# Attention kernel: the blocks that ScalarE copies move from the row-score banks into the ring of score banks

## What is computed

```python
A1 = einsum('bhqd,bhkd->bhqk', Q1, K1) * scaling      # 16 heads, head part of 16 values
A2 = einsum('bhqd,bhkd->bhqk', Q2, K2) * scaling
attn = softmax(A1) - lamb * softmax(A2)
out = einsum('bhqk,bhkd->bhqd', attn, V)
out = layernorm(out.reshape(B, S, DIM) @ Wo) * gamma + beta
```

## Time and profile before

| | us |
|---|---|
| median of 3 runs | 4075.53 (4073.76 to 4076.94) |
| the profiled execution, its own time | 4072.35 |
| its span, from the first to the last instruction | 4070.5 |
| row-score reductions from the prologue's first to the last | 368.6 to 3204 |
| PE busy in the span | 3755.0 |
| DVE busy | 3159.8 |
| ACT busy | 2786.5 |

### The profile page before, as it was taken

One profiled execution on the slowest core, in us unless ns is written; L12 is line 12 of the kernel. 1 busy time (PEld: TensorE's weight loads), 2 busy tenths in 40 slices (PEclk: granted clock), 3 DMA queues, 4 the chain that ended last, 5 costly groups with the idle time before them and its releaser, 6 DMA issues. The chain is left out here.

```text
span 4070.5 us, 63429 instructions
## 1 busy us (share of the span) xinstructions
PE 3755.0 (92%) x23714; PEld 1470.7 (36%) x23714; DVE 3159.8 (78%) x5580; ACT 2786.5 (68%) x3267; POOL 1103.3 (27%) x1520
## 2 busy tenths in 40 slices
PE   6998599999999999999999999999999859899999
PEld 4773122222222222222222222222222236578888
DVE  5457599989999998999999899999999413344444
ACT  3441388888888887888888788888888936522221
POOL 3211013204113212310411231032123157662420
PEclk9997699999999999999999999999999979999999
DMA  5546601111011111111111111111101069832320
GB/s 181 188 162 234 221 29 43 38 49 50 27 48 40 38 48 36 42 38 50 32 37 51 32 38 40 48 32 45 43 22 43 22 235 333 254 115 64 100 83 21
DMA packets 224694, 330.88 MB, mean 81 GB/s; under 512 B 29298, under 2 KB 165237, under 8 KB 219781
## 3 DMA queue, kind: packets, MB, share of 16 engines
q1 hardware_dynamic: 173988, 244.61, 18.5%
q0 software_dynamic: 18432, 50.36, 3.8%
q10 hardware_dynamic: 31968, 31.85, 2.4%
HBM read 169.34 MB, written 156.34 MB: 80 GB/s over the span
## 5 line engine op out<-in xcount | busy, mean ns | idle before, releaser
L1616 DVE TENSOR_REDUCE arena<-psum 128x1 f32<-128x512 f32 x4096 | 2558.5, 681 | 218.3 <-PE psum L1282 200.9
L1470 ACT ACTIVATE arena<-psum,exp_scale 128x1024 f32<-128x1024 f32 x2048 | 2157.7, 1110 | 298.8 <-PE psum L1320 288.9
L1282 PE MATMUL psum<-arena 48*128 48x512 f16 x4096 | 1314.1, 394 | 157.9 <-ACT arena L1430 55.9
L1336 PE MATMUL psum<-arena 128*32 128x512 f32 x8200 | 1107.1, 612 | 1.2 <-ACT arena L1470 0.6
L1282 PEld LDWEIGHTS psum<-arena 48*128 48x128 f16 x4096 | 317.1, 93 | 1808.4 <-DVE arena L1616 1487.0
L1320 PE MATMUL psum<-arena 50*128 50x512 f16 x4096 | 901.7, 384 | 15.9 <-ACT arena L1470 9.2
L1510 POOL TENSOR_TENSOR arena<-arena 128x16 f32<-128x16 f32 x129 | 28.4, 220 | 2123.7 <-DVE arena L1626 2123.7
L991 ACT ACTIVATE mix_arena<-psum,mix_arena 128x1024 f32<-128x1024 f32 x64 | 71.3, 1114 | 329.6 <-DVE mix_arena L1011 329.6
L1336 PEld LDWEIGHTS psum<-arena 128*32 128x32 f32 x8200 | 162.2, 108 | 258.0 <-issue 256.5
L1320 PEld LDWEIGHTS psum<-arena 50*128 50x128 f16 x4096 | 214.0, 95 | 94.1 <-ACT arena L1470 79.4
L894 POOL DMA_INDIRECT mix_arena<-scratch_sorted_y,mix_arena x192 | 181.7, 946 | 235.6 <-PE psum L946 169.1
(11 more groups left out here) (168 smaller groups left out, 3315.4 us busy)
## 6 DMA issues: line engine op xcount, KB each, us to landing
arena<-scratch_split SPq DMA_DIRECT2D x762, 64.0 KB
scratch_split<-route_arena SPq DMA_DIRECT2D x64, 512.0 KB, 2.8
scratch_sorted_x<-arena ACTq DMA_DIRECT2D x60, 512.0 KB, 7.4
leaf_arena<-scratch_sorted_x SPq DMA_DIRECT2D x60, 512.0 KB, 5.8
scratch_sorted_y<-leaf_arena SPq DMA_DIRECT2D x60, 512.0 KB, 4.1
leaf_arena<-in_leafw SPq DMA_DIRECT2D x3, 5128.0 KB, 18.9
arena<-in_x SPq DMA_DIRECT2D x18, 512.0 KB, 4.7
scratch_sum<-arena SPq DMA_DIRECT2D x18, 512.0 KB, 3.0
```

The costliest lines, as they stand in the source:

```text
L1282: nc.tensor.matmul(aux_bank[bank], ring[at, slot, 0, m, qt * P:(qt + 1) * P], ring[at, slot, 1, m, c * CH:(c + 1) * CH], start=True, stop=True
L1336: last = nc.tensor.matmul(value_bank[32 * j:32 * j + 32, :], vaug[:, batch % 2, kt, 2 * pair + j % 2, :], prob[:, step % 2, j, :], start=k ...
L1470: nc.scalar.activation(prob[:, step % 2, 2 * h:2 * h + 2, :], score[:, 2 * h:2 * h + 2, :], ACT.Exp, scale=exp_scale[:, s % 2, s // 2:s // ...
L1616: nc.vector.tensor_reduce(halfmax[:, odd, 2 * m + h, qt, c:c + 1], aux_bank[bank], AX.X, ALU.max).then_inc(bank_used[bank], 1)
```

## The change

The extras leave the ring of three banks. Every exp of a pair and every extra becomes an "item"; the items are numbered in the order in which ACT takes them, and item g is put in slot g mod 2. A slot is one of the two pairs of score banks; an extra uses the first bank of the pair. Item g may be filled when item g - 2 has been read (`wait_slot`). So the pair of banks of m = 0 and m = 1 is no longer fixed, and alternates after each extra. The three banks `aux_bank` hold row scores alone: row score r goes to bank r mod 3 and waits for row score r - 3. The two semaphores `score_full`, `extra_full` become `item_full`, and ACT's reads of either kind count in `item_read`. The order of the instructions on each engine stays: in a step scores 0, row 0, scores 1, row 1, values, row 2, extras, row 3.

```diff
-    score_full, exp_done = sem("score_full"), sem("exp_done")
+    item_full, item_read = sem("item_full"), sem("item_read")
...
-    aux_half = [a.bitcast(F16) for a in aux_bank]
+    item_bank = [ps[:, 2 * n * CH:(2 * n + 1) * CH] for n in range(2)]
+    item_half = [a.bitcast(F16) for a in item_bank]
...
+    item_keys = [("shift", 0)]
+    row_start = [MAXIMA + 4 * AHEAD]
+    for n in range(SETS):
+        i, s = divmod(n, PER_BATCH)
+        for step in range(STEPS):
+            item_keys += [("exp", n, step, 0), ("exp", n, step, 1)]
+            item_keys += [(kind, n, step, number) for kind, number in extras(s, step, i == LAST)]
+            row_start.append(row_start[-1] + len(rows(s, step, i == LAST)))
+    item_keys += [("end", kind, number) for kind, number in EPILOGUE]
+    item_at = {key: g for g, key in enumerate(item_keys)}
+
+    def wait_slot(eng, g):
+        eng.wait_ge(item_read, g + 1)
+
+    def wait_full(eng, g):
+        eng.wait_ge(item_full, g + 2)
+
+    def wait_item(eng, g):
+        eng.wait_ge(item_read, g + 3)
+
+    def wait_row_bank(eng, r):
+        eng.wait_ge(bank_used[r % AUX], r // AUX + 1)
...
             def scores(i, s, step, m):
                 c, kt = step // TT, step % TT
-                g = 2 * (STEPS * s + step)
+                g = item_at["exp", i * PER_BATCH + s, step, m]
+                slot = g % 2
...
-                pe.wait_ge(exp_done, i * SCORES + (g + m + 1))
+                wait_slot(pe, g)
                 for h in (1, 0):
...
-                    last = nc.tensor.matmul(score[:, 2 * m + h, :], ...
+                    last = nc.tensor.matmul(score[:, 2 * slot + h, :], ...
-                last.then_inc(score_full, 1)
+                last.then_inc(item_full, 1)
...
-            def use(i, k, s, step, kind, number):
-                bank = k % AUX
-                wait_free(pe, k)
+            def extra(i, s, step, kind, number):
+                n = i * PER_BATCH + s
+                g = item_at[kind, n, step, number]
+                wait_slot(pe, g)
...
                         scores(i, s, step, 0)
-                        if early:
-                            use(i, k, s, step, *todo[0])
+                        row(0)
                         scores(i, s, step, 1)
-                        if early:
-                            use(i, k + 1, s, step, *todo[1])
+                        row(1)
...
-                        for n in range(early, len(todo)):
-                            use(i, k + n, s, step, *todo[n])
-                        k += len(todo)
+                        row(2)
+                        for kind, number in extras(s, step, tail):
+                            extra(i, s, step, kind, number)
+                        row(3)
```

More of the change, by code:

```diff
@@ L1134, in rows @@
         return [] if tail and target >= PER_BATCH else [("max", first + n) for n in range(4)]
[L1136 to L1142, removed]
     PROLOGUE = [("max", 0, n) for n in range(MAXIMA)] + [("max", 1, n) for n in range(2 * AHEAD)] + \
@@ L1148, in attention_stage, with wait_row_read, shift_item, o_item @@
     LAST = BATCH - 1
[L1149 to L1177, removed]
+    item_keys = [("shift", 0)]
[16 more added lines that the diff above has]
+        eng.wait_ge(bank_used[r % AUX], r // AUX + 1)
+    def wait_row_read(eng, r):
+        eng.wait_ge(bank_used[r % AUX], r // AUX + 2)
+    def shift_item(n):
+        return item_at["shift", 0] if n == 0 else item_at["shift", n - 1, SHIFT_STEP, 0]
+    def o_item(n, c):
+        return item_at["o", n, 5 if c else 11, c]
+    def group_item(i, kind, h, number):
+        s, step = GROUP_PLACES[f"{kind}{h}"][number]
+        return item_at[f"{kind}{h}", i * PER_BATCH + s, step, number]
     def group_end(i, h, kind):
-        places = GROUP_PLACES[f"{kind}{h}"]
-        return place(i, *places[-1], f"{kind}{h}", len(places) - 1)
+        return group_item(i, kind, h, len(GROUP_PLACES[f"{kind}{h}"]) - 1)
     with nc.Block() as block:
@@ L1224, in _ @@
             load_set(2)
-            wait_read(sp, PROLOGUE.index(("shift", 0, 0)))
+            wait_item(sp, shift_item(0))
             place_shift(0)
@@ L1255, in body @@
                     if n + 1 < SETS:
-                        wait_read(sp, place(i, s, SHIFT_STEP, "shift", 0))
+                        wait_item(sp, shift_item(n + 1))
                         place_shift((n + 1) % RING)
@@ L1361, in use @@
                 elif kind == "o":
-                    turn_o(number, i * (2 * PER_BATCH) + (2 * s + (0 if number else 1)), bank)
+                    turn_o(number, 2 * n + (0 if number else 1), g % 2)
                 elif kind in ("turn0", "turn1"):
-                    turn_group(i, int(kind[-1]), number, bank)
-                elif kind in ("out0", "out1"):
+                    turn_group(i, int(kind[-1]), number, g % 2)
+                else:
                     h = int(kind[-1])
[L1367 to L1374, removed]
+                    wait_item(pe, group_item(i, "turn", h, number // 2))
+                    groups[h].project(nc, item_bank[g % 2], number).then_inc(item_full, 1)
@@ L1376, in body, with row @@
             def body(i, tail):
-                k = START[i]
                 for s in range(PER_BATCH):
                     for step in range(STEPS):
-                        todo = uses(s, step, tail)
-                        early = 2 if rows(s, step, tail) else 0
+                        target = row_target(s, step)[0]
+                        first = row_start[STEPS * (i * PER_BATCH + s) + step]
+                        todo = rows(s, step, tail)
+                        def row(n):
+                            if n < len(todo):
+                                number = todo[n][1]
+                                if number == 0:
+                                    pe.wait_ge(slot_in[target % RING], 16 * LOADS * ((i * PER_BATCH + target) // RING + 1))
+                                wait_row_bank(pe, first + n)
+                                row_scores(number, target % RING, (first + n) % AUX)
@@ L1445, in read_group @@
                         act.wait_ge(groups[h].stored, i * 16 + 1)
-                    groups[h].read_projected(nc, aux_bank[bank], number).then_inc(bank_used[bank], 1)
+                    groups[h].read_projected(nc, item_bank[slot], number).then_inc(item_read, 1)
             act.wait_ge(lam_dots, 1)
             nc.scalar.activation(lam_exp, lam_dot, ACT.Exp).then_inc(lam_exps, 1)
-            act.wait_ge(extra_full, 1)
-            read_shift(0, PROLOGUE.index(("shift", 0, 0)) % AUX)
-            def read(i, s, kind, number, bank):
+            wait_full(act, shift_item(0))
@@ L1461, in body @@
             def body(i, tail):
-                k = START[i]
                 for s in range(PER_BATCH):
+                    n = i * PER_BATCH + s
                     for step in range(STEPS):
[L1465 to L1470, removed]
+                        act.wait_ge(value_done, i * VALUES + (STEPS * s + step + 1))
+                        for m in range(2):
+                            g = item_at["exp", n, step, m]
+                            wait_full(act, g)
+                            nc.scalar.activation(prob[:, step % 2, 2 * m:2 * m + 2, :], score[:, 2 * (g % 2):2 * (g % 2) + 2, :],
@@ L1476, in body @@
                             copy_values(i, s - 1, 1)
[L1477 to L1481, removed]
+                        for kind, number in extras(s, step, tail):
+                            g = item_at[kind, n, step, number]
+                            wait_full(act, g)
+                            read(i, s, kind, number, g % 2)
             for i in range(BATCH):
@@ L1626, in invert @@
                 nc.vector.reciprocal(linv[:, c], osum[:, c, :, :, HD]).then_inc(inverse_ready, 1)
-            for k, (kind, n, number) in enumerate(PROLOGUE):
-                if not is_row(kind):
+            row = 0
+            for kind, n, number in PROLOGUE:
+                if kind == "shift":
                     continue
-                dve.wait_ge(rows_full, rows_before[k] + 1)
-                read_max(n, number, k % AUX)
+                dve.wait_ge(rows_full, row + 1)
+                read_max(n, number, row % AUX)
```

138 lines of the change are left out of this document (74 added, 64 removed).

## The result

The changed kernel takes 4111.28 us (median of 4 runs, 4108.88 to 4115.11) against 4074.65 us before (4 runs, one more than in the table above). The ratio is 1.0091, 95% interval 1.0075 to 1.0107: slower by 37 us, where 36 and a median of 4111 were forecast. The profiled execution spans 4107.0 us against 4070.5.

A forecast was written before the change was run, and what follows sets the result against it. DVE was taken to set the pace, with PE's chain counting around extras. Extras +39.8 us and prologue -4 gave +36 on 4075.5: a median of 4111 us, own range 4098 to 4124, overall range 4078 to 4130.

The forecast's parts named there:

- What sets the pace: Attention stage: DVE sets the pace; around extras PE's chain delays it; plain steps stay 2.49 us, DVE waits about 39 more.
- The wait moves one place forward: PE's step after an extra: scores 1, not row 1, wait for ACT's copy; row 1 runs 0.28 us after it.
- Rival 1: Steps after extras: the freed banks win, row 1 no longer waits for a copy; 4039 us in all; chance 8%.
- The price of one extra: Row 1 after an extra: +0.12 us per "o", 0.11 projected, 0.22 turned block or shift; sum 39.8 us.
- The prologue: End of prologue: 43.70 us stall ahead of 14 reductions goes, scores start 5 us earlier, half clock takes 1: -4 us.
- Rival 4: The clock falls at shifts: 81 us more, 4192; with a few such places, 4125 to 4150; chance 7%.
- The rule of the Trainium skill: PE's idle before scores 1 of a shift, 0.7 us: small idles between groups cycling through PSUM banks can make the clock oscillate.
- Rival 2: No net change: DVE slack takes up 0.1 to 0.2 us, leaving prologue and some shifts; 4071 to 4083; chance 7%.

The follow-up runs named there:

- experiment 1: Changed kernel with row score 1 ahead of scores 1 in PE's order in each step behind an extra: 4069.93 us, ratio to before 0.9993.
- experiment 4: Kernel before, old shared ring, with row score 1 ahead of scores 1 in each step behind an extra: 4114.59 us, ratio 1.0103.
- experiment 5: Changed kernel with row score 1 ahead of scores 1 only in steps behind a shift or turned block: 4094.27 us, ratio 1.0051.
- experiment 6: Changed kernel with DVE's statistics of an output group cut up and spread over the row scores of two steps: 4083.2 us, ratio 1.0026.
- experiment 7: Kernel before with the first shift behind all prologue row scores and DVE's statistics spread: 4044.12 us, ratio 0.9928.
- experiment 3: Kernel before, shared ring kept, with the first shift behind all 96 row scores of the prologue: 4066.84 us, ratio 0.9985.
- experiment 2: Changed kernel with row score 1 and values ahead of scores 1 in each step behind an extra: 4116.86 us, ratio 1.0109.
- experiment 8: Changed kernel with row score 1 ahead of scores 1 after every extra and DVE's statistics spread: 4046.45 us, ratio 0.9937.

## Why the prediction was right

**What sets the pace.** DVE, and PE's chain only around extras. Right: a plain step still takes 2.49 us (`values` at 1649.07 and 1651.56), and the delays of the chain arrived in DVE's waits, 47.5 us more over the steps, where about 39 were forecast.

**The wait moves one place forward, with scores 1 now behind it.** Right. The changed kernel shows it; experiment 1 takes it away in the new ring and experiment 4 brings it about in the old one, by about 41 us each time. Rival 1 (the freed banks win) is out: with scores 1 out of the way (experiment 1) the row scores did use the freed banks, and the gain over the kernel before was still none but the prologue's. PE's own matmuls fill the chain at an "o" or a projected block, and at a shift `values` still stand behind scores 1 and so behind the copy.

**The price of one extra.** 0.12 at an "o" (measured 0.12, from the copy's start to row 1), 0.22 at a shift (measured 1668.01 - 1667.79 = 0.22 between the two that swapped). By kind, experiment 5 measured 17 us for shifts and turned blocks where 18 stood, and experiments 1 and 5 together leave 4094.3 - 4069.9 = 24 us for "o" and projected blocks where 15.0 + 6.2 = 21 stood. With the statistics spread in both, the steps of experiments 6 and 7 differ by 2746.1 - 2704.8 = 41.3 us, where 39.8 stood. The single extras can be read at the start: 5.94 us ahead of the kernel before up to step 3, the reductions are 5.72 ahead behind the turned block of step 3, 5.50 behind that of step 4 and 5.38 behind the "o" of step 5, so 0.22, 0.22 and 0.12 each. One detail was off: of a shift's 0.2 us only 0.02 came at row 2 (0.62 for 0.60, not 0.82), and the rest one reduction earlier, where DVE now runs dry at row 1. Its three reductions ahead of that wait take 2.08 us with the gap, and took 1.89 before:

```profile
1653.38 1.89 DVE L1616 TENSOR_REDUCE arena<-psum 128x1 f32<-128x512 f32 x3 [0.17 <-PE psum L1282]
```

0.19 + 0.02 = 0.21: the sum is the same.

**The prologue.** -4 was forecast: 5 for the earlier start, less 1 for the half clock. In the trace the first reduction of the steps comes 6.4 us earlier, 1.35 of it from the earlier end of the zero fills, and the 5.0 that are left are those estimated. The half clock, which now ended at about 469.1 and not at 474.5, took back only 0.4: the third reduction comes 5.95 us earlier.

```profile
475.35 8.15 DVE L1616 TENSOR_REDUCE arena<-psum 128x1 f32<-128x512 f32 x13 [0.98 <-PE psum L1282]
```

```profile
469.40 8.15 DVE L1635 TENSOR_REDUCE arena<-psum 128x1 f32<-128x512 f32 x13 [1.41 <-PE psum L1289]
```

The same two reductions come 4.8 and 4.2 us earlier in experiment 3's trace, whose fills ended 0.24 us late. So the term was too small by about 0.5 us, and the rest of the gap is the accident of the fills. Experiment 3's runs, -6.5 with an interval from -2 to -10, can't tell this.

**What the sum lacked.** The 4.5 us at the statistics. The prediction said that nothing changes there. Experiment 6 shows that the waits behind the statistics hang on that block and go with it. Their growth isn't an accident of one execution: it comes and goes with the order on PE, as these traces show (one execution each; the steps run from their first reduction to the last, the waits are counted as in experiment 6).

| kernel | steps, us | of them at half clock | DVE's waits behind the statistics |
|---|---|---|---|
| before | 2731.3 | 65 | 21.4 |
| experiment 3 | 2731.0 | 65 | 20.6 |
| experiment 1 | 2732.0 | 61 | 20.7 |
| changed | 2775.5 | 82 | 25.9 |
| experiment 4 | 2776.1 | 89 | 26.8 |
| experiment 5 | 2759.3 | 82 | 27.0 |

Where "o" and projected blocks have their price, the half clock lasts longer (6.8 us at 8 to 10 places in place of 4 to 6). Which of the two, the later start of PE's work or the longer half clock, brings about the other isn't shown. The 4.5 us cancelled with what the prologue gave beyond its 4 us, 1.35 of it by accident, and with the 1.3 us of the later stages, so the total came closer than its terms deserve.

**Rival 4, the clock falling at shifts.** It didn't: the window around the shift shown above has 1.00, and each of the 15 drops of the granted clock among the changed kernel's steps begins within 4 us after the last instruction of a statistics block.

```profile
1666.00:1669.00 3.00, 2.44 (x24) 0.81 (x23) 2.55 (x4) 2.77 (x4) 0.00 (x0) 1.00 0.00 1
```

PE stands idle 0.56 us in it. The rule of the Trainium skill weighed in the prediction (TensorE: Matmul & The Clock Gate, "A second HAM failure mode: psum-queue depth-cycling") tells of small idles that come again and again; for pauses of this size, one per set, the trace doesn't bear it out. At the statistics the clock does fall, but there PE stands still once, for 1.42 or 2.81 us.

**Rival 2, no net change,** is out by the interval.

## What to carry to other kernels

Removing a wait from one instruction says little as long as the same event still holds one that stands ahead of it in the engine's order: write down what is queued behind the wait before and after, and count the work that used to run during it. On an engine that works in order, put whatever doesn't depend on the awaited event ahead of the wait, but only as much as the wait is long: 1 us of work put ahead of a wait of 0.1 to 0.56 us made a consumer late (experiment 2). Which banks the blocks use cost nothing by itself here; what stood behind the wait cost 40 us. And look at long blocks of small instructions on the engine that sets the pace: cutting them up gave 23 to 28 us here, of which some 3 are the long instruction's own, 1.15 us in place of 1.56 at eight places.

## What the runs showed of the hardware that wasn't expected

A block of small instructions on DVE cost PE its clock, at 15 of the 16 blocks in the kernel before and in the changed one: half clock for 3.4 or 6.8 us each time. In either kernel the blocks that held PE up for 2.81 us did so at 8 of 8 places, those that held it up for 1.42 us at 7 of 8 (in experiment 2, with other work around them, at 1 of 8). With the block cut up the longest standstill is 0.84 us, at eight places; the clock fell at two of them in experiment 6 and at none in experiments 7 and 8. Pauses of 0.56 us, at each shift of the changed kernel, never showed such a drop.
